# A selective-scan and expert kernel: w made for two states at a time in the two row halves of TensorE, and most C products given to GpSimd

## The reference

```
xn = layernorm(x)                              # over 256 channels d
B_t = xn @ W_B.T ; C_t = xn @ W_C.T            # 16 states n
dt  = softplus((xn @ W_dt1.T) @ W_dt2.T + b)   # per token and channel
A   = -exp(log_A) ; A_bar = exp(dt * A)        # per token, d, n
h_t = A_bar * h_(t-1) + (A_bar - 1)/A * xn * B_t
y_t = sum over n of h_t * C_t ; x = x + y + D_skip * xn
then: layernorm, softmax over 8 experts, the best expert's
      gelu(x @ W1[e] + b1[e]) @ W2[e] + b2[e], added to x
```

## Time and profile before

| | us |
|---|---|
| median of 3 runs | 805.61 |
| profiled execution | 804.56 |
| its span, first to last instruction | 802.8 |
| busy in the span: TensorE matmul | 749.1 (93%) |
| VectorE | 546.2 (68%) |
| GpSimd | 533.0 (66%) |
| ScalarE | 461.3 (57%) |

### The profile page before, as it was taken

One profiled execution on the slowest core, in us unless ns is written; L12 is line 12 of the kernel. 1 busy time (PEld: TensorE's weight loads), 2 busy tenths in 40 slices (PEclk: granted clock), 3 DMA queues, 4 the chain that ended last, 5 costly groups with the idle time before them and its releaser, 6 DMA issues. The chain is left out here.

```text
span 802.8 us, 17303 instructions
## 1 busy us (share of the span) xinstructions
PE 749.1 (93%) x5642; PEld 695.0 (87%) x5643; DVE 546.2 (68%) x914; ACT 461.3 (57%) x941; POOL 533.0 (66%) x654
## 2 busy tenths in 40 slices
PE   7899999999999997998998975969999999999993
PEld 5799999999899897898897975959999999999992
DVE  6889998989989989989789963353333334333430
ACT  3777898887888876876866753422332233223330
POOL 2799999989989986999898863552333343334420
PEclk9799999999999999998999987989999999999997
DMA  8666643233323331642844448341111111111000
GB/s 290 198 220 233 259 135 105 94 132 106 124 76 106 134 106 54 122 112 60 124 90 54 165 137 283 34 54 40 50 46 53 39 44 49 43 55 53 23 9 0
DMA packets 44375, 82.49 MB, mean 103 GB/s; under 512 B 6280, under 2 KB 14733, under 8 KB 44304
## 3 DMA queue, kind: packets, MB, share of 16 engines
q1 hardware_dynamic: 38288, 68.98, 29.2%
q0 software_dynamic: 6016, 12.61, 6.4%
HBM read 70.41 MB, written 13.91 MB: 105 GB/s over the span
## 5 line engine op out<-in xcount | busy, mean ns | idle before, releaser
L574 POOL TENSOR_TENSOR w_sb<-w_sb,Csb 128x512 f32<-128x512 f32 x182 | 231.7, 1275 | 41.2 <-DVE w_sb L1110 28.5
L921 PE MATMUL WW<-b_sb,xin 128*128 128x129 f32 (+1 forms) x1536 | 206.3, 284 | 8.3 <-DVE w_sb L1130 5.8
L921 PEld LDWEIGHTS WW<-b_sb,xin 128*128 128x128 f32 x1536 | 190.2, 197 | 24.0 <-issue 13.8
L812 ACT ACTIVATE dt<-WW,b1c 128x128 f32<-128x128 f32 x312 | 89.1, 369 | 191.8 <-PE WW L1008 191.8
L1110 DVE TENSOR_TENSOR_SCAN w_sb<-WW,hlast,w_sb 128x512 f32<-128x512 f32 x138 | 173.3, 1271 | 17.6 <-PE WW L921 17.2
L741 ACT ACTIVATE w_sb<-dt,negA 128x512 f32<-128x512 f32 x256 | 170.9, 710 | 18.7 <-DVE w_sb L1110 15.0
L1024 PE MATMUL misc<-w_sb,dt 128*128 x624 | 146.8, 390 | 9.1 <-issue 9.1
L634 POOL DMA_INDIRECT y_out<-CbX,ocol x39 | 46.8, 1201 | 150.5 <-DVE CbX L1418 149.9
L1024 PEld LDWEIGHTS misc<-w_sb,dt 128*128 128x128 f32 x624 | 119.5, 197 | 25.9 <-issue 10.1
L939 PE MATMUL YY<-sm,w_sb 128*128 128x128 f32 x1024 | 129.3, 276 | 0.1
L1008 PE MATMUL WW<-z,xin 128*128 128x128 f32 x624 | 120.7, 275 | 0.0
(11 more groups left out here) (214 smaller groups left out, 880.0 us busy)
## 6 DMA issues: line engine op xcount, KB each, us to landing
w_sb<-c_rows SPq DMA_DIRECT2D x86, 256.0 KB, 3.7
CbX<-c_rows SPq DMA_DIRECT2D x42, 256.0 KB, 3.5
w_sb<-w_in SPq DMA_DIRECT2D x20, 512.0 KB, 5.7
token_rows<-row SPq DMA_DIRECT2D x8, 1024.0 KB, 5.0
w_sb<-w_in SPq DMA_DIRECT2D x24, 256.0 KB, 6.6
xin<-x_in SPq DMA_DIRECT2D x8, 512.0 KB, 4.1
w_sb<-x_in SPq DMA_DIRECT2D x7, 512.0 KB, 10.0
b_sb<-b_in SPq DMA_DIRECT2D x1, 774.0 KB, 4.7
```

What stands on the lines that cost most here:

```text
L574: eng.tensor_tensor(hc[g % NHC], hb_of(g), Csb[i % NCS][:, :], ALU.mult).then_inc(s_hcp, 1)
L812: g = eng.activation(hT[u % 2][:, j * P:(j + 1) * P], hps[u % 2][:, j * P:(j + 1) * P], ACT.Gelu, bias=b1c[u][:, j:j + 1])
L921: mm = eng.matmul(bank_of_w[:, i * P:i * P + width], x_rows[:, i, h * P:(h + 1) * P], bands[m % NR][:, i, 0:width], start=(i == 0), stop=( ...
```

## The change

An item's place is renumbered: `place(g)` makes 4 consecutive items out of two states n, n+1 and both halves h, in the order (n, h0), (n+1, h0), (n, h1), (n+1, h1). Two consecutive items (a *unit*, two states of one half h) now share 1024 columns of PSUM (two banks), with the two states in alternate columns, so that one matmul makes w for both: its moving operand is a band for 64 tokens, 65 times 2 = 130 columns, and its contraction runs over 64 rows of the array. Tokens 0 to 63 of each 128 are in the lower rows and the others in the upper, and consecutive matmuls alternate between the halves of the array and between the two banks. `make_w(m, part)` has part 0 (4 matmuls and one of 2 columns, for the edge between the banks) and part 1 (4 matmuls), with an `add_y` behind each; part 1 waits for the end of part 0. There are two w areas instead of four banks: unit m waits until both items of unit m-2 have been scanned (and, on VectorE, multiplied with C). GpSimd's `make_band` makes one band per two states. Each chunk has 1 unit on VectorE (`VECTOR_UNITS`: 2 in the first chunk, 3 in the last), where `VECTOR_N` had 6, 4, 4, 4, 4, 5, 5 and 5 pairs. All hops stand at the end of their pair.

```diff
-VECTOR_N = [(1, 3, 5, 8, 11, 13)] + [(1, 5, 8, 11)] * 4 + [(1, 3, 5, 8, 11)] * 2 + [(1, 4, 7, 10, 13)]
+VECTOR_UNITS = [(1, 9)] + [(6,)] * 6 + [(1, 7, 13)]
-BAND = P + 1
-NR, NA, NH, NHC, NCS, NW, NB = 4, 4, 8, 8, 3, 4, 6
+HALF = P // 2
+BAND = 2 * (HALF + 1)
+NR, NA, NH, NHC, NCS, NW, NB = 3, 4, 8, 8, 3, 4, 6
+def place(g):
+    q, j = divmod(g, ITEMS)
+    return q, j // 4 * 2 + j % 2, j // 2 % 2
...
+        def unit(m):
+            return WW[:, m % 2 * 1024:(m % 2 + 1) * 1024]
+        def w_of(g):
+            return unit(g // 2).rearrange("p (t s) -> p s t", s=2)[:, g % 2, :]
...
-            def make_band(m):
+            def make_band(pair):
...
-                wait(eng, s_wv, KD * (m - NR + 1))
-                eng.tensor_tensor(bands[m % NR], col("band").unsqueeze(1).to_broadcast([P, TI, BAND]),
-                                  brow[q % B][:, :, N + n:N + n + 1].to_broadcast([P, TI, BAND]), ALU.mult)\
-                   .then_inc(s_R, 1)
+                wait(eng, s_wv, 4 * (pair - NR + 1))
+                eng.tensor_tensor(bands[pair % NR].rearrange("p i (t s) -> p i t s", s=2),
+                                  col("band").unsqueeze(1).unsqueeze(3).to_broadcast([P, TI, HALF + 1, 2]),
+                                  brow[q % B][:, :, N + 2 * p:N + 2 * p + 2].unsqueeze(2)
+                                  .to_broadcast([P, TI, HALF + 1, 2]), ALU.mult).then_inc(s_R, 1)
...
-                for i in range(TI):
-                    width = min(BAND, TC - i * P)
-                    mm = eng.matmul(bank_of_w[:, i * P:i * P + width], x_rows[:, i, h * P:(h + 1) * P],
-                                    bands[m % NR][:, i, 0:width], start=(i == 0), stop=(i == TI - 1),
-                                    skip_group_check=True)
-                mm.then_inc(s_wv, 1)
+                def product(r, k, at=0, width=BAND, start=False):
+                    rows = slice(HALF * r, HALF * r + HALF)
+                    a = 2 * (P * k + HALF * r) + at
+                    return eng.matmul(to[:, a:a + width], x_rows[rows, k, h * P:(h + 1) * P],
+                                      band[rows, k, at:at + width], start=start, stop=not start, skip_group_check=True)
+                if part == 0:
+                    if h == 0:
+                        eng.wait_ge(s_R, pair + 1)
+                    if m >= 2:
+                        if pooled(2 * m - 4):
+                            eng.wait_ge(s_h, 2 * m - 2)
+                        else:
+                            eng.wait_ge(s_hc, vector_before(2 * m - 2))
+                    product(0, 0, start=True)
+                    product(1, 2, start=True)
+                    product(0, 1)
+                    product(1, 3, width=2 * HALF)
+                    product(1, 1, at=2 * HALF, width=2).then_inc(s_wf, 1)
+                else:
+                    eng.wait_ge(s_wf, m + 1)
+                    product(0, 2)
+                    product(1, 0)
+                    product(0, 3)
+                    product(1, 1, width=2 * HALF).then_inc(s_wv, 2)
...
-                    if n < 2 or n in VECTOR_N[q]:
-                        add_y(KD * m - 4)
-                        add_y(KD * m - 3)
-                        if n in at:
-                            fill(*at[n])
-                        make_w(KD * m + 4)
-                        make_w(KD * m + 5)
-                    else:
-                        make_w(KD * m + 4)
-                        if n in at:
-                            fill(*at[n])
-                        make_w(KD * m + 5)
-                        add_y(KD * m - 4)
-                        add_y(KD * m - 3)
+                    make_w(m + 2, 0)
+                    add_y(KD * m - 4)
+                    make_w(m + 2, 1)
+                    add_y(KD * m - 3)
+                    if n in at:
+                        fill(*at[n])
...
-                    if g % KD and not pooled(g) and KEPT[g // KD]:
-                        keep_h(g)
-                    if g and not pooled(g - 1):
+                    if g % KD and not pooled(g):
                         make_hc(g - 1)
+                        if KEPT[g // KD]:
+                            keep_h(g)
+                        make_hc(g)
```

More of the change, by code:

```diff
@@ L29 @@
 ITEMS = N * KD
-VECTOR_N = [(1, 3, 5, 8, 11, 13)] + [(1, 5, 8, 11)] * 4 + [(1, 3, 5, 8, 11)] * 2 + [(1, 4, 7, 10, 13)]
-POOLED = [g // KD % N not in VECTOR_N[g // ITEMS] for g in range(ITEMS * NQ)]
+VECTOR_UNITS = [(1, 9)] + [(6,)] * 6 + [(1, 7, 13)]
+POOLED = [g // KD % N not in VECTOR_UNITS[g // ITEMS] for g in range(ITEMS * NQ)]
 POOL_BEFORE = [0, *accumulate(POOLED)]
@@ L48 @@
 EPS = 1e-5
-SMALL = dict(ident=P, logA=KD * N, wr=KD * E, wcd=KD * CBD, wdt2=D, skip=D, band=BAND, last=1,
+SMALL = dict(ident=P, logA=KD * N, wr=KD * E, wcd=KD * CBD, wdt2=D, skip=D, band=HALF + 1, last=1,
              b1=E * KH, tri=P, e_less8=E, e_base=E, tok0=NT, j128=32, tile_no=MT, br=E)
@@ L215, in build @@
         Csb = [Csbs[:, i * TC:(i + 1) * TC] for i in range(NCS)]
-        bands = [b2_sb[:, i * TI * BAND:(i + 1) * TI * BAND].rearrange("p (i t) -> p i t", t=BAND)
-                 for i in range(NR - 1)] + [sb("band3", [P, TI, BAND])[:, :, :]]
+        bands = [b2_sb[:, i * TI * BAND:(i + 1) * TI * BAND].rearrange("p (i t) -> p i t", t=BAND) for i in range(NR)]
         brow = [sb(f"brow{b}", [P, TI, 2 * N])[:, :, :] for b in range(B)]
@@ L458, in refill_rings @@
                 for g in range(end - 2 * NHC, end + 4):
-                    if g == end - NA - 3:
+                    if g == end - 2:
                         eng.wait_ge(s_wv, end)
@@ L464, in refill_rings @@
                         refill(AT + g % NA)
-                    if g < end and g % KD and g // KD + NB >= N * NQ and CT + g // KD % NB < RINGS:
-                        wait(eng, s_hc, vector_before(g + 1))
-                        wait(eng, s_Cs, pool_before(g + 1))
-                        refill(CT + g // KD % NB)
+                    if g < end and place(g)[2]:
+                        c = place(g)[0] * N + place(g)[1]
+                        if c + NB >= N * NQ and CT + c % NB < RINGS:
+                            wait(eng, s_hc, vector_before(g + 1))
+                            wait(eng, s_Cs, pool_before(g + 1))
+                            refill(CT + c % NB)
                     if g < end and pooled(g) and pool_before(g) + NH >= POOL_BEFORE[-1]:
@@ L641, in _ @@
             row_products(0, 0)
-            for m in range(3):
-                make_band(m)
+            for pair in range(2):
+                make_band(pair)
             start_ahead()
@@ L905, in fill, with make_w @@
                 mm.then_inc(s_full, 1)
-            def make_w(g):
-                if g >= ITEMS * NQ:
+            def make_w(m, part):
+                if m >= N * NQ:
                     return
-                m, h = divmod(g, KD)
-                x_rows, bank_of_w = xin[m // N % B], bank[g % NW]
-                if h == 0:
-                    eng.wait_ge(s_R, m + 1)
-                if g >= NW:
-                    if pooled(g - NW):
-                        eng.wait_ge(s_h, g - NW + 1)
-                    else:
-                        eng.wait_ge(s_hc, vector_before(g - NW) + 1)
-                for i in range(TI):
-                    width = min(BAND, TC - i * P)
-                    mm = eng.matmul(bank_of_w[:, i * P:i * P + width], x_rows[:, i, h * P:(h + 1) * P],
-                                    bands[m % NR][:, i, 0:width], start=(i == 0), stop=(i == TI - 1),
-                                    skip_group_check=True)
-                mm.then_inc(s_wv, 1)
+                pair, h = divmod(m, 2)
+                x_rows, band, to = xin[m // N % B], bands[pair % NR], unit(m)
+                def product(r, k, at=0, width=BAND, start=False):
[22 more added lines that the diff above has]
+                    product(1, 1, width=2 * HALF).then_inc(s_wv, 2)
             def add_y(g):
@@ L977, in _ @@
             eng.wait_ge(s_skip, 2)
-            for g in range(4):
-                make_w(g)
+            for part in range(2):
+                for m in range(2):
+                    make_w(m, part)
             fill(FIRST[-1], 0)
@@ L1100, in scan @@
                 pi = pool_before(g)
-                if q % NC and h == 0:
+                if q % NC and g % KD == 0:
                     if pooled(g - ITEMS):
@@ L1457 @@
     skip[N] = a["attn_D_skip"]
-    band = np.zeros((P, BAND), f)
-    band[one, one] = 1.0
-    band[one, one + 1] = -1.0
+    band = np.zeros((P, HALF + 1), f)
+    band[one, one % HALF] = 1.0
+    band[one, one % HALF + 1] = -1.0
     parts = dict(
```

60 lines of the change are left out of this document (29 added, 31 removed).

## The result

The changed kernel takes 917.89 us (median of 4 runs, 904.3 to 932.1) where the kernel before took 805.51 beside it: ratio 1.131, 95% interval 1.116 to 1.145. A median here is over all executions, while a ratio leaves out those more than 1.5% above the fastest of their kernel, so the two can differ (917.89 over 805.51 is 1.140). The forecast was 796.

What follows compares the result with a forecast made beforehand. TensorE was taken to bound the middle chunks, with four engines nearly full. Middle chunks -4.0, first +0.5, six and seven -4.5, last -2.0 made -10.0 us: 794.6 profiled, 796 for the median, range 791 to 801 (chance 0.42).

Steps and rivals of the forecast that it cites:

- TensorE's term: w in row halves: a unit takes 2.64 us against 2.70, two shape round trips included; a middle chunk 53.2 us.
- rival B: TensorE: shape changes cost more with real operands, 0.30 us each instead of 0.175; 847 us in all; chance 0.08.
- GpSimd, VectorE, ScalarE: Busy time per middle chunk after the change: GpSimd 50.1 us, VectorE 46.6, ScalarE 50.4, all beside TensorE's 53.2.
- rival C: GpSimd: the new band is as slow as a product, 1.6 us more per chunk; 804 us in all; chance 0.14.
- The waits: Hand-over of units: 2.2 us from scans' end to w fits VectorE's 2.4 us of other scans, hops included.
- Rival A: Whole-unit hand-over stalls TensorE and VectorE in turn, 7% on a middle chunk, 56.9 us; 819 in all; chance 0.22.
- The prediction's own sign of error: A middle chunk over 55 us would mean hand-over trouble or dearer shape changes; under 52.5, cheaper or hidden ones.
- It is real work at 2.4 GHz: TensorE in the second chunk before the change: 54.2 us busy of 54.4, at clock 1.00.
- Chunks six and seven: Gaps around VectorE's pairs mostly go; GpSimd longest at 113.7 us, 118.1 with gaps, against 122.6: 4.5 less.
- the sign of error given for them: The prediction is wrong if chunks six and seven don't shorten.

Runs made afterwards that it cites:

- f2: Changed kernel with hops first in their pair, both parts of w side by side, and y ahead of w in each chunk's first two pairs: 803.83 us, ratio 0.999.
- g2: f2 with a y again between the two parts of w from the third pair of each chunk on: 817.31 us, ratio 1.007.
- e6: Changed kernel with hops first in their pair, then both parts of w, then both y's: 818.86 us, ratio 1.008.
- Experiment 3: Kernel before the change (whole rows, four banks) with its hops moved to the end of their pair: 848.02 us, ratio 1.040.
- experiment 1: Changed kernel with each hop at the start of its pair instead of the end, nothing else: 833.45 us, ratio 1.027.
- e1: The kernel of experiment 1: changed kernel with each hop at the start of its pair: 833.45 us, ratio 1.027.
- experiment 4: Kernel before the change, with w of either item waiting until both items of the pair two places ahead have left their banks: 816.87 us, ratio 1.015.
- experiment 7: w on all 128 rows (w values differ), in the changed kernel: 899.56 us, ratio 1.118; with hops first as well: 843.17 us, ratio 1.038.
- f3: f2 with three units instead of one on VectorE in the seventh chunk: 811.4 us, ratio 0.997.
- e2: Changed kernel with every w matmul on all 128 rows of the array (w values differ): 899.56 us, ratio 1.118.
- b1: The kernel of experiment 3: kernel before the change with its hops at the end of their pair: 848.02 us, ratio 1.040.
- b2: Kernel before the change with the C products divided between VectorE and GpSimd as in the changed kernel: 836.99 us, ratio 1.039.
- b3: The kernel of experiment 4: kernel before the change with w handed over in whole units: 816.87 us, ratio 1.015.
- e5: Changed kernel with hops first in their pair and w on all 128 rows (w values differ): 843.17 us, ratio 1.038.
- g1: f2 with the w matmuls on all 128 rows instead of 64 (w values differ): 841.76 us, ratio 1.043.
- e4: Changed kernel with the C products divided as before the change, 26 more units on VectorE: 914.72 us, ratio 1.137.

## Why the prediction was wrong

**TensorE's term** was right for a unit: 2.59 us at 2.4 GHz (forecast 2.64). The price of the changes of shape held, and rival B (0.30 each) is false. That a chunk of f2 takes 53.1 us (forecast 53.2) is partly luck. f2 has one round trip per unit where the sum has two, and TensorE is busy for only 50.5 of the 53.2 us, so this chunk is not TensorE's alone. With two round trips (g2) it is 53.7, of which 51.5 are busy. The second round trip costs so little because part 1 waits openly for part 0 when they stand side by side. By the timelines a unit is 2.47 us that way (last section) and 2.59 with a y between, 0.12 less, where e6's expectation had 0.35 - 0.25 = 0.10; the open wait takes the place of most of the change of shape. Of the 14 x 0.12 = 1.7 us a chunk shows 0.6, as it has waits as well.

**GpSimd, VectorE, ScalarE** were right within 0.7 us per chunk (third chunk 49.8, 46.8, 49.7 against 50.1, 46.6, 50.4). The band with operands in runs of two elements takes 1067 ns, not 1273: rival C is false. The failure lies in how the engines wait for each other, and in the clock.

**"The waits"** is the step that failed. It counted 2.2 us from scans to w against 2.4 of scanning, called that a fit, and let the hops in "because VectorE has 46.6 us of work in 53". It looked at how full an engine is, not at what its next instruction waits for. Three instructions of other engines (`tail` on VectorE, `vlast` on ScalarE, and the sum of rows behind the last y) want a result that had been moved behind a w, and VectorE's next scans, which a later w wants, are queued behind `tail` and the sum of rows. Experiment 3 puts the moved hops at 33 us even without any other change, experiment 1 at 84 in the changed kernel. Three changes of order take the whole ratio of 1.131 away, with units, split and row halves left in: hops first 0.104 (e1), the parts of w side by side 0.019 (e6), y first in two pairs 0.009 (f2).

Rival A had the sign and the mutual wait, but named "a hop stands ahead of w" as the cause; it was the hop *behind* w. Its price of 7% came from one chunk of the kernel before, in which the hops still stood ahead of the pair's w's or between them. The hand-over that A is named for is 12 us by experiment 4, near its sum of 13, but f2, in which whole units are handed over too, is level. The prediction's own sign of error, a middle chunk over 55 us, came true (70 to 83 us), mostly for a cause that it doesn't list.

**"It is real work at 2.4 GHz"**, read before the change, was carried over to the kernel after it, and this failed as well: the sum has no term for the clock. After the change TensorE has idle gaps and less of the array at work, and 265 us of the scan phase (196 to 225 in the other executions) are at 1.2 GHz, where a unit costs 4.63 us instead of 2.59. By experiment 7 this adds some 20 us to the 64 of the knots. In f2, without most of the waits, the first and the sixth chunk lose at a clock of 0.83 what the others gain.

**Chunks six and seven** were to lose 4.5 us by fewer gaps. In f2 they take 125.1 us against 122.6 before, with GpSimd's load as forecast (113.5 us), so the sign of error given for them came true. The clock is the likely reason, and it isn't shown: f2 has 0.83 and 0.92 there, and f3, with 0.94 in both, takes 119.5 us, near the forecast's 118.1, but f3 has less for GpSimd to do as well.

## What to carry to other kernels

When a statement is moved on an in-order engine, list every consumer of its result and what is queued behind that consumer; if the moved statement now stands behind a wait for one of those, the wait runs in a circle, and it costs several us each time, however empty the engines are. And a saving on TensorE which leaves part of the array unused is to be priced at both of its clock levels, since it may itself bring the lower one: here the mended kernel (f2) ends level with the one before, with 1.1 to 1.3 us less in its second to fourth chunks, at 2.4 GHz, and as much lost in those with a lower clock. Before and after such a change, compare the clock chunk by chunk, and not in one execution alone: the same kernel had 40 to 72 us at 1.2 GHz from one execution to the next.

## What the runs showed of the hardware

TensorE fell to 1.2 GHz in f2 while its records followed each other without a gap. Its timeline from 335 us, and two stretches around the fall (columns as above):

```profile
335.17 1.61 PE L936 MATMUL WW<-b_sb,xin 64*128 64x130 f32 x18
336.71 1.09 PE L972 MATMUL YY<-sm,w_sb 128*128 128x128 f32 x8
337.64 1.85 PE L903 MATMUL misc<-sm,xnrT 128*128 128x8 f32 x16
339.42 1.61 PE L936 MATMUL WW<-b_sb,xin 64*128 64x130 f32 x18
340.96 1.77 PE L972 MATMUL YY<-sm,w_sb 128*128 128x128 f32 x8
342.66 2.74 PE L936 MATMUL WW<-b_sb,xin 64*128 64x130 f32 x18
345.33 1.97 PE L972 MATMUL YY<-sm,w_sb 128*128 128x128 f32 x8
347.23 2.07 PE L892 MATMUL misc<-sm,z 17*128 17x256 f32 x4
```

```profile
334.20:341.20 7.00, 6.88 (x66) 5.69 (x65) 4.65 (x5) 6.10 (x11) 6.80 (x9) 1.00 0.48 67
341.20:365.10 23.90, 23.67 (x123) 19.71 (x122) 13.93 (x18) 14.83 (x26) 18.91 (x23) 0.50 0.31 89
```

It then stayed at 1.2 GHz for 23.9 us with matmul records over 23.67 of them. A unit of w with its two y's takes 337.64 - 335.17 = 2.47 us before the fall and 347.23 - 342.66 = 4.57 in it. In the kernel before the fall at 308.8 us came behind idle time, as this stretch of it shows (5.83 us of 8.80 busy):

```profile
300.00:308.80 8.80, 5.83 (x51) 5.36 (x49) 8.47 (x18) 6.34 (x11) 5.59 (x7) 1.00 0.10 39
```

**How long it stays down.** In the changed kernel and in its copy with whole rows (e2), both with their knots, one stretch each at 1.2 GHz:

```profile
140.30:184.60 44.30, 39.89 (x202) 31.72 (x200) 19.25 (x22) 21.30 (x37) 23.35 (x28) 0.50 0.18 60
153.60:160.40 6.80, 6.16 (x27) 5.86 (x28) 1.67 (x2) 2.78 (x4) 3.66 (x4) 0.50 0.00 0
```

TensorE is busy for 90% of either. In the profiles of all seven kernels with whole rows (before, b1, b2, b3, e2, e5, g1) no stretch at 1.2 GHz in the scan phase is longer than 6.9 us. With row halves the longest are 44.4 us (changed), 54.6 (e4), 30.7 (e1) and 23.9 (f2). With whole rows and the same order (g1) the phase has 10 us at 1.2 GHz, with row halves 60; with hops first 31 and 186; in the changed kernel's order 75 and 265; and the estimates for the other executions don't overlap in any of the three pairs, in which the only edit is the number of rows.

**What stands ahead of a fall.** The halves alone don't bring the clock down: f2's second to fifth chunks, 214 us of them, are at 1.00. Just ahead of its fall at 341.2 us stands a hop, the router's product at 337.64: eight matmuls of 8 columns (L903, 16 records), once per chunk. This goes for every fall that has 3.3 us or more of records on end ahead of it. The twelve profiles of kernels with row halves have 20 of them, and in each this hop began 1.6 to 3.7 us before. In e1 the falls at 183.5, 251.8, 320.1 and 449.8 us stand behind hops at 181.3, 248.3, 316.7 and 446.4, in g2 those at 235.5, 290.1 and 416.4 behind 232.2, 286.6 and 413.1, in f3 the one at 231.3 behind 227.6. The clock doesn't fall behind each such hop (in f2 it holds at 121.7, 174.8, 227.9 and 280.8), and with whole rows it never did so without a gap: there every fall in the scan phase came behind idle time. So the y between the parts need not be what tips the fifth chunk of g2. No run moves this hop or makes it wider between row halves, and what it contributes is not shown; it is the next thing to test.

The Trainium skill ("TensorE: Matmul & The Clock Gate", "Part 1: The HAM clock gate") says that the low clock is the default and that activity releases it. The rows agree where TensorE idles. They also show that busy records are not all there is to it: with row halves the clock fell and stayed down under records without a gap (23.67 us of 23.9), with whole rows it did neither. What it is in the halves that makes the difference, the runs don't tell.
